# Gram and score products on dense 64-row blocks, with other orders of the input scalings and of the waits on PSUM

## The reference, cut to what matters

```python
x = x + _L0_conv_ref(_gn(x), ...)
t = _to_tokens(x)                      # (4, 256, 64)
t = t + _L1_attn_ref(_ln_t(t), Wq, Wk, Wv, Wo)
# _L1_attn_ref, 8 heads of 64 channels:
attn = jnp.einsum('bhnd,bhne->bhde', qh, kh)          # 64 x 64 scores per head and image
mu = attn.mean(axis=(2, 3), keepdims=True)
var = attn.var(axis=(2, 3), keepdims=True)
attn = jax.nn.softmax((attn - mu) * jax.lax.rsqrt(var + EPS), axis=3)
ctx = jnp.einsum('bhde,bhne->bhdn', attn, vh)
return ctx.transpose(0, 3, 2, 1).reshape(b, n, c * h) @ Wo
```

## Time and profile before

| | us |
|---|---|
| median of 3 runs | 67.06 (66.84 to 68.09) |
| the profiled execution | 66.78 |
| its span, first to last instruction | 65.0 |
| PE busy | 51.6 (79%) |
| DVE busy | 37.2 (57%) |
| ACT busy | 34.5 (53%) |
| POOL busy | 20.0 (31%) |
| mean granted clock of TensorE, as a share of 2.4 GHz | 0.971 |

### The profile page before, as it was taken

The page is one execution under the profiler, slowest core; times in us unless marked ns, Lnnn a source line. Parts: engine busy times, 40 slices in busy tenths (PEclk is TensorE's granted clock), DMA queues, the critical chain, the costliest instruction groups (busy, mean ns, idle before and its releaser), DMA issues.

```text
span 65.0 us, 1827 instructions
## 1 busy us (share of the span) xinstructions
PE 51.6 (79%) x651; PEld 36.8 (57%) x657; DVE 37.2 (57%) x162; ACT 34.5 (53%) x88; POOL 20.0 (31%) x51
## 2 busy tenths in 40 slices
PE   2999998899698925999996899999698569981420
PEld 0323555897587613899876686667233649930110
DVE  3888863979838473315381731991355581658930
ACT  0713297594246641037599403899875399226700
POOL 6998071000493387000000000000005588950000
PEclk9999999999999999999999999999999999999855
...
DMA packets 5673, 3.47 MB, mean 53 GB/s; under 512 B 2912, under 2 KB 5216, under 8 KB 5664
## 3 DMA queue, kind: packets, MB, share of 16 engines
...
q10 hardware_dynamic: 288, 0.44, 1.8%
q0 software_dynamic: 176, 0.27, 1.6%
...
HBM read 3.10 MB, written 0.26 MB: 52 GB/s over the span
## 4 chain that ended last, share of the span: by engine, by line
PE 44%; DVE 20%; ACT 10%; issue 10%; POOL 8%; POOLq 4%; DVEq 0%; ACTq 0%
PE ps L894 40%; ACT f L459 2%; ACT L555 2%; POOLq L302 2%; PE ps L929 2%; DVE f_st L621 2%; POOL w1s L312 2%; DVE ts L767 1%; POOL b2t L428 1%; POOL b2t L430 1%; POOLq L126 1%; DVE xp L690 1%; DVE pv L808 1%; DVE yc L713 1%; ACT t2T L559 1%
## 5 line engine op out<-in xcount | busy, mean ns | idle before, releaser
L894 PE MATMUL ps<-zeros 128*128 128x512 bf16 x45 | 14.8, 442 | 1.5 <-DVE zeros L663 1.2
L894 PEld LDWEIGHTS ps<-zeros 128*128 128x128 bf16 x51 | 5.0, 108 | 6.2 <-issue 1.4
L312 POOL COPY w1s<-fw 64x128 f32 x4 | 1.1, 296 | 23.9 <-issue 23.2
L894 PE MATMUL ps<-w2s,h 128*128 128x64 f32 x32 | 3.8, 276 | 0.5 <-POOL w2s L421 0.5
L894 PEld LDWEIGHTS ps<-w2s,h 128*128 128x128 f32 x32 | 3.6, 192 | 0.9 <-ACT h L575 0.9
L575 ACT ACTIVATE h<-ps,b1s 128x256 f32<-128x256 f32 x8 | 3.1, 479 | 1.1 <-PE ps L894 1.1
L894 PE MATMUL ps<-yc,taps 128*128 128x32 bf16 x128 | 3.4, 176 | 0.4 <-DVE yc L713 0.4
L894 PEld LDWEIGHTS ps<-yc,taps 128*128 128x128 bf16 x128 | 3.3, 96 | 0.6 <-issue 0.6
L1188 PE MATMUL ps<-consts,n 128*128 128x128 f32 x4 | 1.5, 366 | 2.5 <-ACT n L459 1.4
L894 PE MATMUL ps<-wt,xw 128*32 128x64 f32 x128 | 2.6, 222 | 0.7 <-issue 0.7
L894 PE MATMUL ps<-ts,t 128*128 128x128 f32 x8 | 1.7, 293 | 1.7 <-DVE ts L767 1.6
...
## 6 DMA issues: line engine op xcount, KB each, us to landing
...
```

Source lines behind the costliest of these rows:

```text
L312: eng.tensor_copy(w1s[r, t_, k, :].unsqueeze(1), fw1[r, bass.ds(mine[k], 1), :]).then_inc(copied, 1)
L894: return pe.matmul(dst, lhsT, rhs, start=start, stop=stop)
```

## The change

The layout of the Gram tile becomes dense: `gram` holds the 64 x 64 block of image l on partition half l, for both t_, so that it is 64 rows by 128 columns per half and needs no zeros. wk is dense too (each half holds all heads, no zero blocks), as are wks and wkm. The product with wq is now one matmul per (half of the heads, l), 64 rows by 128 columns of weights, each into a bank of its own; the product with wkm goes into the tail of the banks gq10 and gq11. The scores are 32 matmuls of 64 x 64 in place of 8 of 128 x 128, and the row parts 16 in place of 8. ScalarE, in place of VectorE, copies gm. The row parts are squared in two instructions, and rsq has a zeroed form with 128 rows.

In the input scaling, tiles 1 and 3 are scaled whole by VectorE in one tensor_tensor each, tiles 0 and 2 by ScalarE and GpSimd in halves. GpSimd makes wqc ahead of its scalings. `written` no longer counts o0 to o3, rows and eT (UNCOUNTED). Three residual pieces are issued ahead of the values and one after them, three matmuls of zeros go (one ahead of eT, two ahead of the values), one matmul of zeros takes the place of the residual piece between the halves of m, and ScalarE copies eT after prob.

```diff
-    ("gram", "V"), ("gq0", "V"), ("gq1", "A"), ("gm", "V"), ("attn0", "V"), ("attn1", "V"), ("eT", "A"), ("avar", "A"),
-    ("o0", "O"), ("o1", "O"), ("o2", "O"), ("v00", "V"), ("v01", "V"), ("v10", "V"), ("v11", "V"), ("o3", "O"), ("m", "V"),
+    ("gram", "V"), ("gq00", "V"), ("gq01", "V"), ("gq10", "A"), ("gq11", "A"), ("a00", "V"), ("a01", "V"), ("a10", "V"), ("a11", "V"),
+    ("avar", "A"), ("rows", "A"), ("eT", "A"), ("o0", "O"), ("v00", "V"), ("v01", "V"), ("v10", "V"), ("v11", "V"),
+    ("o1", "O"), ("o2", "O"), ("o3", "O"), ("m", "V"),
 SHARED = {"m": "v00"}
+UNCOUNTED = ("o0", "o1", "o2", "o3", "rows", "eT")
+WRITTEN = {name: sum(1 for other, _ in CHUNKS[:j + 1] if other not in UNCOUNTED) for j, (name, _) in enumerate(CHUNKS)}
...
-            eng.wait_ge(written, INDEX[name] + 1)
+            eng.wait_ge(written, WRITTEN[name])
...
-            zero(wk[:, :, :, :], "wk")
-            zero(wks[:, :, :], "wks")
...
+            pool.tensor_tensor(wk[:, :, :], wk[:, :, :], wkm[:, :].unsqueeze(2).to_broadcast([P, HEADS, C]), ALU.subtract).then_inc(made["wkc"], 1)
...
-            for i in range(NQ - 1):
-                j = 2 * i + 1
-                wait_read(pool, f"t{i}")
-                pool.wait_ge(made["e_inverse"], i + 1)
-                pool.tensor_scalar(ts[:, j, :], t[:, j, :], evr[:, j:j + 1], None, ALU.mult).then_inc(made["scaled_by_pool"], 1)
...
+            for i in (0, 2):
+                j = 2 * i + 1
+                wait_read(pool, f"t{i}")
+                pool.wait_ge(made["e_inverse"], i + 1)
+                pool.tensor_scalar(ts[:, j, :], t[:, j, :], evr[:, j:j + 1], None, ALU.mult).then_inc(made["scaled_by_pool"], 1)
...
-            wait_read(act, "t1")
-            scale_input(1, 2)
...
-            wait_read(act, "t3")
-            scale_input(3, 7)
+            wait_read(act, "t2")
+            scale_input(2, 4)
...
+            wait_chunk(act, "gq11")
+            two = HOME["gq10"]
+            copy(gq[:, :, HH:, :], ps[:, two:two + 2, 0:HH * C]).then_inc(made["gq_by_scalar"], 1)
+            copy(gm[:, :, :], ps[:, two:two + 2, HH * C:HH * C + HEADS]).then_inc(read_a, 2)
...
-            wait_chunk(act, "eT")
-            copy(eT[:, :, :], bank("eT")).then_inc(read_a, 1)
...
+            act.wait_ge(made["tokens_transposed"], 1)
+            copy(eT[:, :, :], bank("eT")).then_inc(read_a, 1)
...
+                dve.tensor_tensor(ts[:, j:j + 2, :], t[:, j:j + 2, :], evr[:, j:j + 2].unsqueeze(2).to_broadcast([P, 2, C]), ALU.mult).then_inc(made["scaled_by_vector"], 1)
...
+            input_scale(1)
+            input_stats(3)
             input_variance(2)
             input_inverse(2)
-            input_stats(3)
             input_moments(3)
-            input_scale(2, 4)
             input_variance(3)
             input_inverse(3)
-            input_scale(3, 6)
-            dve.wait_ge(const["gram"], 1)
+            input_scale(3)
...
-                    ins = mm(dst, dsb[:, i, g, :], wpg[:, g, :, :], False, False)
-                ins.then_inc(written, 1)
+                    mm(dst, dsb[:, i, g, :], wpg[:, g, :, :], False, False)
...
             for i in range(2):
-                dst = begin(f"gq{i}")
+                for l in range(2):
+                    r = slice(l * C, (l + 1) * C)
+                    ins = mm(begin(f"gq{i}{l}")[:, 0:HH * C], gram[r, :, :], wq[r, i * HH * C:(i + 1) * HH * C])
+                    if i == 0:
+                        ins.then_inc(written, 1)
+            pe.wait_ge(made["wkm"], 1)
+            for l in range(2):
+                r = slice(l * C, (l + 1) * C)
+                mm(bank(f"gq1{l}")[:, HH * C:HH * C + HEADS], gram[r, :, :], wkm[r, :]).then_inc(written, 1)
+            pe.wait_ge(made["wkc"], 1)
+            for i in range(2):
+                if i == 0:
+                    wait_read(pe, "gq01")
+                else:
+                    pe.wait_ge(made["gq_by_scalar"], 1)
+                dsts = [begin(f"a{i}{t_}") for t_ in range(BH)]
+                for q in range(HH):
+                    for l in range(2):
+                        for t_ in range(BH):
+                            r = slice(t_ * C, (t_ + 1) * C)
+                            ins = mm(dsts[t_][l * C:(l + 1) * C, q * C:(q + 1) * C], wk[r, i * HH + q, :], gq[r, l, i * HH + q, :])
+                            if q == HH - 1 and l == 1:
+                                ins.then_inc(written, 1)
+            dst = begin("avar")
+            dsts = [dst, begin("rows")]
+            pe.wait_ge(made["wqc"], 1)
+            wait_read(pe, "gq11")
+            for hd in range(HEADS):
                 for t_ in range(BH):
-                    ins = mm(dst[:, t_ * HH * C:(t_ + 1) * HH * C], gram[:, t_, :], wq[:, i * HH * C:(i + 1) * HH * C])
-                ins.then_inc(written, 1)
-            dst = begin("gm")
-            pe.wait_ge(made["wks"], 2)
-            pe.wait_ge(made["wkm"], 1)
-            for t_ in range(BH):
-                ins = mm(dst[:, t_ * HEADS * 2:(t_ + 1) * HEADS * 2], gram[:, t_, :], wkm[:, :, :])
-            ins.then_inc(written, 1)
-            pe.wait_ge(made["wkc"], 2)
-            for i in range(2):
-                wait_read(pe, f"gq{i}")
-                dst = begin(f"attn{i}")
-                for q in range(HH):
-                    hd = i * HH + q
-                    ins = mm(dst[:, q * P:(q + 1) * P], wk[:, hd, :, :], gq[:, :, hd, :])
-                ins.then_inc(written, 1)
-            dst = begin("avar")
-            pe.wait_ge(made["wqc"], 1)
-            wait_read(pe, "gm")
-            for hd in range(HEADS):
-                c0 = 2 * HEADS * BH + hd * 4
-                ins = mm(dst[0:C, c0:c0 + 4], wqc[:, hd * C:(hd + 1) * C], gm[:, :, hd, :])
+                    r = slice(t_ * C, (t_ + 1) * C)
+                    o = slice(hd % 2 * C, hd % 2 * C + C)
+                    c0 = ROW0 + hd // 2 * 2
+                    ins = mm(dsts[t_][o, c0:c0 + 2], wqc[r, hd * C:(hd + 1) * C], gm[r, :, hd])
             ins.then_inc(made["row_parts"], 1)
-            pe.wait_ge(made["scores_squared"], 1)
-            keep_warm("eT", WARM["scores"])
             pe.wait_ge(made["e"], 1)
             eT_ = begin("eT")
             for i in range(NQ):
                 ins = pe.transpose(eT_[:, i * P:(i + 1) * P], e[:, 2 * i:2 * i + 2, :], ident)
-            ins.then_inc(written, 1)
-            pe.wait_ge(made["row_parts_squared"], 1)
+            ins.then_inc(made["tokens_transposed"], 1)
+            pe.wait_ge(made["row_parts_squared"], 2)
             for l in range(2):
-                mm(dst[l * C:(l + 1) * C, 0:HEADS * BH], blk_row, rsq[:, :, :, l], True, False)
+                mm(dst[l * C:(l + 1) * C, 0:HEADS * BH].rearrange("p (i t q) -> p i t q", i=2, t=BH), blk_row,
+                   rsq[:, :, :, :, l].rearrange("p t (i k) r -> p i t (k r)", i=2), True, False)
             pe.wait_ge(made["score_sums"], 2)
-            mm(dst[:, 0:HEADS * BH], blk, ast[:, :, :], False, True).then_inc(written, 1)
-
-            residual(0)
-            residual(1)
-            wait_read(pe, "avar")
-            keep_warm("o2", WARM["deviations"])
-            wait_read(pe, "attn0")
-            keep_warm("o2", WARM["softmax"])
+            mm(dst[:, 0:HEADS * BH], blk, ast[:, :, :, :], False, True).then_inc(written, 1)
+
+            for i in range(3):
+                residual(i)
...
-                    residual(2 + i // 2)
                     if i == 0:
+                        residual(3)
                         dst = begin("m")[:, BANK - BH * C:]
+                    else:
+                        keep_warm("fT", WARM["values"])
```

129 lines of the change are left out of this document (63 added, 66 removed).

## The result

The changed kernel takes 63.21 us, the median of 4 executions (62.81 to 63.97), against 66.95 us (66.34 to 68.09, 4 executions) for the kernel before on the same chip: a ratio of 0.945, with a 95% interval of 0.9325 to 0.9575. That is faster, and the forecast was 63.3. Medians are over all executions, while ratios and intervals leave out the slow ones, which most kernels here have now and then. The profiled execution took 62.81 us with a span of 60.7 (66.78 and 65.0 before). PE was busy for 49.1 us (81%), DVE 35.7, ACT 34.4, POOL 17.3.

What follows compares the result with a forecast made beforehand. TensorE had the largest busy share, but three stretches of the chain mattered: input scaling, products and scores, softmax and values. Terms -1.0 - 1.7 - 1.05 = -3.75 from 66.78 gave 63.0, plus 0.28 made 63.3; range 62.3 to 65.2.

Steps and rivals of the forecast that it cites:

- Term A: Input scaling, up to the product with wq: the new split lets the last scaling and Gram product go sooner; -1.0 us.
- The rule of the lock: Input scaling: GpSimd's port lock also holds VectorE's two-input operations; Term A would be near -0.7, the whole 0.3 us worse.
- Term B: Gram copy to the product with the sums: row halves overlap in the wq product and score passes get cheap; -1.7 us.
- The price of the score passes: Scores: 16 ns per pass as in wvT, 0.5 us per half plus tail; far bound 60 ns per pass.
- TensorE is not late: Before the product with the sums: row parts, eT and ScalarE's squares of them end by 29.1, product at 29.27.
- Term C: Root, table load and softmax: the 1.28 us load stays on the chain and hides three residual pieces; 0 us.
- Term D: Values to the copy of m: uncounted o0 to o3 and moved residual pieces make m sooner; -1.05 us.
- The rest: Everything else, such as wk's load and GpSimd's earlier loads: nothing before 15 us waits for them; 0 us.
- drain at a changed array shape: TensorE at changes of array shape: no drain seen; by the skill's rule two more changes would add some 0.4 us.
- The partial case: Rival: row halves don't overlap in the wq product and GpSimd holds up the new scaling; 64.8 us, chance 0.13.
- the clock fall in the new stretch: Rival: TensorE's clock falls to 1.2 GHz from about 27 us until m; 69.3 us, chance 0.03; short fall 0.06.

Runs made afterwards that it cites:

- e1: Changed kernel with the old split of the input scalings over ScalarE, GpSimd and VectorE, and wqc last on GpSimd; 65.0 us, too uneven for a ratio.
- e9: Changed kernel with GpSimd's wqm and wqc between its two input scalings, wqc timed to meet VectorE's wide scaling; 64.1 us, ratio 0.964.
- e4: Changed kernel with the score passes issued in runs on one quarter of the array instead of alternating quarters; 64.0 us, ratio 0.961.
- e12: The changed kernel again without an edit, on the third chip; 63.07 us, ratio 0.940.
- e8: Changed kernel without the square root of the score variances, the Exp table loaded right behind the squares of the row parts; 62.72 us.
- e6: Kernel before, with only o0 to o3 no longer counted in `written` and the order of issue unchanged; 66.28 us, ratio 0.997.
- e7: Kernel before, with only the order of the residual pieces and the matmuls of zeros around them changed, old counting; 65.41 us, ratio 0.980.
- e11: Old input scaling as in e1, with five more matmuls of zeros between the Gram products; 64.01 us, ratio 0.963.

## Why the prediction was right

**Term A, -1.0 forecast, -1.21 measured** (1.16 by e1). GpSimd's scaling of tile 2 did fall on the variance of tile 3 (22.23 and 22.24), but cost 0.03 and not the 0.1 allowed for (0.19, where its likes take 0.16). One step was wrong and its error was made good by the next: VectorE was to have the squares' sums 1.90 behind the statistics of tile 1 and took them at 2.20 (21.71), as before (2.19), because in the new order the statistics of tile 3 (21.43, 0.36 us) come first; the prediction had put those behind. So the last scaling began at 3.22 where 3.25 was said. The larger part of the gain over e1, 0.69 of 1.16, is that wqc no longer meets a scaling; against the kernel before that part is 0.42 (0.68 for 0.26). The rule of the lock, by which A would have been -0.7, is right about the operation (e9: 0.97 for 0.29) and would have been wrong about this kernel, because in the changed order the wide scalings (20.93 and 22.73, 0.29 each) meet no GpSimd operation at all: GpSimd is idle from 20.00 to 22.23 and from 22.68 to 23.26. Whether a GpSimd scaling would hold a wide one, no run shows.

**Term B, -1.7 forecast, -1.79 measured.** By its steps, from the start of the product with wq: VectorE's copy +0.76 forecast, +0.81 measured; ScalarE's +1.56, +1.30; the first squares +2.36, +2.38; the product with the sums +4.43, +4.35. ScalarE was sooner, since the product with wkm took 0.32 and ran beside the last wq passes, but that gained nothing, as the scores waited for VectorE's copy and began at +1.61 (+1.56 forecast). The price of the score passes, taken from wvT at 16 ns and not from the 60 ns of gm with wqc, was the choice that decided the term; e4 shows what stands behind it: about 38 ns per pass in runs (2.4 us for 63 distances) and 15 alternating. "TensorE is not late" was true in the profiled execution (row parts at 28.18, sums at 28.48) and fails in others (e12, by 0.47 us). What is left out of the prediction is the pause itself.

**Term C, 0 forecast, +0.07 measured.** Three residual pieces were hidden, with 0.3 us to spare as worked out (e8).

**Term D, -1.05 forecast, -0.92 measured.** Row sums +0.76 forecast, +0.81 measured; second wo +2.86, +2.99. The first wo came behind the last residual piece as forecast (+2.01, +2.0 forecast). The step that was mis-sized is the one from there to the second wo, taken as TensorE's own work (0.63 and 0.22 for the matmul of zeros): it took 0.98, because the second wo waits for VectorE's second pv, which ends at 34.08. The matmul of zeros cost nothing. That the count gives 0.4 to 0.5 alone is confirmed (0.37 by e6), that it is needed for the whole is not (e7).

**The rest, 0 forecast, -0.44 measured:** 0.35 of it is the shorter "issue" gap ahead of wt with xw, which varies in the same code from none (e7) to 0.91 (e11). It happened to be long in the profile of before and short after; in e12 (19.75) and e9 (19.71) the stage began nearer to the old 19.95.

**Luck in the number.** The mechanism of A, B and D is borne out, but that the median (63.21) lies 0.1 from the forecast is in part luck. A and B gave 0.3 more than forecast and C and D 0.2 less, and the unforecast 0.44 of the first row stands against 0.33 more outside the span. In e12 the five distances sum to 35.75 and not 35.17, which is 3.71 less than before.

**Rivals.** The prediction saw no drain at a changed array shape because the next group starts before the last one ends. That is a weak sign, as the profile models the ends of matmuls. By the starts, the first pass behind a change of shape comes 0.15 to 0.21 us after the last one (32.35 to 32.50 into the residual piece, 33.16 to 33.36 out of it), where most passes inside the piece are 0.11 apart. So the rule of the Trainium skill (TensorEngine Tiling (Array Packing), section Tiling Modes) that a changed mode drains TensorE is neither borne out nor refuted here. The 0.4 us which the prediction put on it were not worked out from a row, and the sum came out without them. The partial case didn't come: row halves do overlap. Nor did the clock fall in the new stretch; where it fell between 20 and 50 us, it was behind the old scaling (0.66 in e1 from 25 to 30 us, 0.67 in e7). So on the clock the new split was no risk, and may be a help.
